# Top-1 expert layer over sorted tokens in groups of 1024 with weights gathered per tile, recurrence summed in PSUM, norm roots on GpSimd

## The reference

```python
px = x @ W_state.T + b_state ; g = sigmoid(x @ W_gate.T + b_gate)      # part 1
state = tanh(px_t + state) ; out_t = g_t * state                        # 256 steps, one after the other
top_id = argmax(x @ gate_w.T) ; score = sigmoid(max(x @ gate_w.T))      # part 2, E = 8 experts, F = 256
for e in range(8):
    xe = where(top_id == e, x * score, 0)
    acc += (silu(xe @ wg[e].T) * (xe @ wu[e].T)) @ wd[e].T
out = shared_swiglu(x) + acc
A = einsum('sbnq,sbnv->bnvq', unit(k), v * w)                           # part 3, 16 heads of 8
out = (einsum('sbnq,bnvq->sbnv', unit(q), A) * r) @ Wo.T + b
```

## Time and profile before

| | us |
|---|---|
| median of 3 runs (4196.43 to 4217.24) | 4210.99 |
| the profiled execution, its own time | 4206.35 |
| its span in the trace | 4204.6 |
| the first stage in it, 0 to the memset | 841 |
| what follows | 3363 |

### The profile page before, as it was taken

How to read it: one execution, slowest core, us unless ns; L and a number is a source line. 1 busy time by engine, 2 the same in 40 slices (tenths; PEclk the granted TensorE clock), 3 DMA queues, 4 the chain that set the end, 5 groups by cost and what they waited for, 6 DMA issues and landing times.

```text
span 4204.6 us, 149958 instructions
## 1 busy us (share of the span) xinstructions
PE 3830.9 (91%) x64432; PEld 2715.8 (65%) x64432; DVE 2923.7 (70%) x5136; ACT 2315.7 (55%) x4220; POOL 2929.8 (70%) x4274
## 2 busy tenths in 40 slices
PE   6989899778999899998999989999899998999997
PEld 3444444357777677776777767777677776777774
DVE  3566665567777677777777777777677776778672
ACT  3222211146666666666666666666666666666662
POOL 0122223288888788887888878888788887888782
PEclk9999999789999999999999999999999999999998
DMA  1000000011111111111111111111111111111110
GB/s 66 3 5 5 6 3 3 15 48 41 37 37 37 49 39 43 38 35 50 39 41 37 38 42 47 39 38 39 41 45 42 38 37 44 41 45 39 41 38 24
DMA packets 96277, 147.02 MB, mean 35 GB/s; under 512 B 27264, under 2 KB 35840, under 8 KB 95488
## 3 DMA queue, kind: packets, MB, share of 16 engines
q1 hardware_dynamic: 95616, 137.42, 13.0%
HBM read 32.46 MB, written 4.19 MB: 9 GB/s over the span
## 4 chain that ended last, share of the span: by engine, by line
PE 57%; POOL 26%; issue 8%; DVE 4%; ACT 2%; DMA 1%; SPq 1%; POOLq 0%; DVEq 0%; ACTq 0%
PE bank L445 12%; POOL m L1339 7%; PE bank L378 5%; PE bank L527 5%; PE bank L516 5%; POOL m L1333 4%; PE bank L489 4%; POOL S L1355 4%; PE bank L465 3%; PE bank L566 3%; POOL S L1347 3%; PE bank L455 3%; PE bank L500 3%; PE bank L393 2%; PE bank L574 2%
## 5 line engine op out<-in xcount | busy, mean ns | idle before, releaser
L445 PE MATMUL bank<-wqkv,xs 128*128 128x512 f32 x3456 | 1139.5, 446 | 16.3 <-DVE m L834 14.6
L1339 POOL TENSOR_TENSOR m<-m 128x512 f32<-128x512 f32 x768 | 966.5, 1279 | 47.6 <-DVE m L834 47.6
L445 PEld LDWEIGHTS bank<-wqkv,xs 128*128 128x128 f32 x3456 | 606.0, 195 | 179.3 <-issue 100.3
L832 DVE TENSOR_TENSOR m<-bank,tab 128x512 f32<-128x512 f32 x768 | 516.8, 673 | 132.5 <-ACT sq L1104 90.0
L844 DVE TENSOR_REDUCE ss<-sq 128x8 f32<-128x512 f32 x768 | 514.5, 677 | 120.4 <-ACT sq L1104 119.4
L834 DVE TENSOR_TENSOR m<-bank,tab 128x512 f32<-128x512 f32 x768 | 522.3, 680 | 35.8 <-POOL m L1339 35.7
L1104 ACT ACTIVATE sq<-bank 128x512 f32<-128x512 f32 x768 | 457.5, 596 | 130.7 <-PE bank L445 111.6
L1347 POOL TENSOR_TENSOR S<-S,nw 128x1024 f32<-128x1024 f32 x192 | 365.2, 1902 | 104.7 <-DVE S L864 104.6
L516 PEld LDWEIGHTS bank<-P,big 64*64 64x64 f32 x24576 | 376.2, 135 | 90.3 <-issue 89.7
L1355 POOL TENSOR_TENSOR S<-S,rs 128x512 f32<-128x512 f32 x384 | 392.9, 1044 | 39.1 <-DVE rs L878 38.8
L1112 ACT ACTIVATE vst<-bank 128x512 f32<-128x512 f32 x384 | 232.9, 606 | 328.2 <-PE bank L445 326.6
(11 more groups left out here) (202 smaller groups left out, 6586.6 us busy)
## 6 DMA issues: line engine op xcount, KB each, us to landing
big<-vst SPq DMA_DIRECT2D x1536, 64.0 KB, 2.0
stage<-in_wqkv SPq DMA_DIRECT2D x36, 256.0 KB, 2.9
tab<-in_tab SPq DMA_DIRECT2D x48, 128.0 KB, 2.2
big<-in_wa SPq DMA_DIRECT2D x1, 3460.0 KB, 12.8
wo<-in_wo SPq DMA_DIRECT2D x6, 512.0 KB, 3.7
big<-in_x SPq DMA_DIRECT2D x8, 256.0 KB, 2.9
keep<-Xr SPq DMA_DIRECT2D x8, 256.0 KB, 2.0
stage<-keep SPq DMA_DIRECT2D x8, 256.0 KB, 3.1
```

Of the source, the lines that this page charges most:

```text
L445: m = eng.matmul(pb[:, :], xt[a], wqkv[:, z, 512 * part:512 * part + 512], start=(n == 0), stop=(n == 2))
L832: eng.tensor_tensor(m1[:, part, :].rearrange("p (h d) -> p h d", d=DH), pv, ct.unsqueeze(1).to_broadcast([P, 8, DH]), ALU.mult)
L1339: eng.tensor_tensor(m1[:, part, :], m1[:, part, :], m2[:, part % 2, :], ALU.add).then_inc(s["g_add"], 1)
```

## The change

Parts 1 to 3 get another program; part 4 is the same.

- The experts work on sorted tokens. For a group of 1024 tokens (two chunks; GR = 4 groups) `rk` ranks them by expert: nine small matmuls (sums over tokens by a matrix of ones and by `below`, a triangle) and 13 small VectorE instructions give each token a slot so that each expert begins on a multiple of 128, in TL = 15 tiles. `xt` turns the tokens to rows and scales them; `sc` scatters them to DRAM by eight indirect DMAs of 128 rows; `lx` loads the sorted rows (SyncE, four DMAs). `wg` gathers the 128x768 weights of one tile's expert by an indirect DMA, into a ring of four; `tx` turns four tiles of tokens back to columns; `ge` is gate and up of two tiles, `he` silu, `ye` the down-projection, `ey` its copy to SBUF, `sy` a store to DRAM, `yg` eight indirect gathers that bring each token its row, and `cb` four matmuls by the identity that add it to the shared expert's output in bank 4. Expert weights are no longer all in SBUF.
- The recurrence has no VectorE part: for each step TensorE puts W_state times the column of x in a bank (`state_in`, 128x16) and adds the last state to it by a matmul with the identity; ScalarE's tanh reads PSUM and adds the bias.
- The root of each layer norm moves to GpSimd (`norm_root`, 12 small instructions), after a ScalarE copy; the widening copy of `fs` moves to ScalarE.
- `chunk_order()` is written anew: 7 rounds r of two halves; in half `now` = 2r or 2r+1 one chunk is in the recurrence, group r-1 in its experts (first half: ranks, scatter, tiles 0 to 5 and the gate of 6 and 7; second half: the rest and `yg`), and the chunks 2(r-2), 2(r-2)+1 in part 3. Each item has a place from -2 to 96, and a step is put in every third place or so.

```diff
-WA, WA_N = columns([("ws", 128), ("wg", 128), ("router", 8), ("sg", 256), ("su", 256), ("sd", 256),
-                    ("eg", E * 256), ("eu", E * 256), ("ed", E * 256)])
+WA, WA_N = columns([("ws", 128), ("wg", 128), ("router", 8), ("sg", 256), ("su", 256), ("sd", 256), ("below", 128),
+                    ("row", 1), ("tiles", 15)])
+GR, TL, PR = NC // 2, 15, 8
+SLOTS = 128 * TL
...
-    for p in range(-2, NC + 2):
-        gather = [
-            [("u", p + 1, 0), ("px", p + 2, 0), ("gu", p, 0), ("n2a", p - 1, 0), ("wv", p - 2, 0)],
-            [("gu", p, 1), ("n2b", p - 1, 0), ("n1a", p + 1, 0), ("wv", p - 2, 1), ("pm", p - 2, 0)],
-            [("gu", p, 2), ("n1b", p + 1, 0), ("wv", p - 2, 2), ("pm", p - 2, 1)],
...
+    for r in range(GR + 3):
+        for half in range(2):
+            e, a = r - 1, 2 * (r - 2)
+            done, now = 2 * r + half - 1, 2 * r + half
+            at = [(-2, "px", now, 0), (22, "pg", now, 0)] if now < NC else []
+            if 0 <= done < NC:
+                at += [(0, "u", done, 0), (3, "n1a", done, 0), (5, "n1b", done, 0), (8, "n1c", done, 0), (10, "ra", done, 0), (12, "xt", done, 0)]
+            if 0 <= e < GR and half == 0:
+                at += [(15, "rk", e, 0), (17, "sc", e, 0), (18, "lx", e, 0)] + [(18, "wg", e, j) for j in range(4)]
...
+            if 0 <= e < GR:
+                at += [(x[0], "wg", e, j) for x in at if x[1] == "ye" for j in (2 * x[3] + 4, 2 * x[3] + 5) if j < TL]
+            if 0 <= a < NC and half == 0:
+                at += [(2, "sh", a, 0), (4, "sh", a, 1), (7, "sd", a, 0), (7, "cb", a, 0), (9, "xr", a, 0), (11, "n2a", a, 0), (14, "n2b", a, 0),
+                       (17, "n2c", a, 0), (19, "fp", a, 0), (21, "fp", a, 1), (23, "fp", a, 2), (25, "fs", a, 0), (27, "fp", a, 3), (30, "fb", a, 0),
+                       (33, "fb", a, 1)]
+                at += [(36 + 8 * j, "wv", a, j) for j in range(8)] + [(45 + 8 * j, "pm", a, j) for j in range(7)]
...
+            taken = 0
+            for place, what, c, j in sorted(at, key=lambda x: x[0]):
+                while now < NC and taken < min(W, W * place // 95):
+                    yield "step", now, 0
+                    taken += 1
+                yield what, c, j
+            if now < NC:
+                yield "rest", now, 0
...
-        wa = big1
+        wa = big1[:, 0:WA_N]
+        wr = [big1[:, WA_N + 768 * i:WA_N + 768 * (i + 1)] for i in range(4)]
...
+                elif what == "lx":
+                    q.wait_ge("d_sc", 128 * (c + 1))
+                    q.wait_ge("p_tx", 4 * c)
+                    for n in range(4):
+                        eng.dma_start(XS[:, 4 * n:min(4 * n + 4, TL), :], rows_of(xsort_d, c, n)).then_inc(s[f"d_xs{n}"], 16)
+                elif what == "sy":
+                    q.wait_ge("a_y", PR * c + 2 * j + 2)
+                    eng.dma_start(rows_of(ysort_d, c, j), Y[:, 4 * j:min(4 * j + 4, TL), :]).then_inc(s["d_ys"], 16)
...
+            def state_in(n):
+
+                c, t = n // W, n % W
+                pe.wait_ge("a_rec", n - 1)
+                eng.matmul(bank[2 + n % 2][:, 0:NB], wa[:, WA["ws"]], bt(xin[c % 2])[:, :, t], start=True,
+                           stop=(n == 0)).then_inc(s["p_px"], 1)
+
+            def steps(c, first, last):
+                for t in range(first, last):
+                    n = W * c + t
+                    if n:
+                        prev = bt(hist[c % 2])[:, :, t - 1] if t else bt(hist[(c - 1) % 2])[:, :, W - 1]
+                        pe.wait_ge("d_kc", 32)
+                        pe.wait_ge("a_rec", n)
+                        eng.matmul(bank[2 + n % 2][:, 0:NB], ident, prev, start=False, stop=True).then_inc(s["p_st"], 1)
+                    if t < W - 1:
+                        state_in(n + 1)
...
+                elif what == "tx":
+                    pe.wait_ge(f"d_xs{j}", 16 * (c + 1))
+                    pb = claim(4)
+                    for n in range(4 * j, min(4 * j + 4, TL)):
+                        m = eng.transpose(pb[:, 128 * (n % 4):128 * (n % 4) + 128], XS[:, n, :], ident)
+                    m.then_inc(s["p_tx"], 1)
+                    vacant[4] = [("a_tx", 4 * c + j + 1)]
+                elif what == "ge":
+                    k = PR * c + j
+                    pe.wait_ge("a_tx", 4 * c + j // 2 + 1)
+                    pg, pu = claim(0), claim(1)
+                    for n in range(2 * j, min(2 * j + 2, TL)):
+                        g = TL * c + n
+                        pe.wait_ge(f"d_w{g % 4}", 16 * (g // 4 + 1))
+                        for pb, w0 in ((pg, 0), (pu, 256)):
+                            for f in range(2):
+                                a = 256 * (n % 2) + 128 * f
+                                m = eng.matmul(pb[:, a:a + 128], wr[g % 4][:, w0 + 128 * f:w0 + 128 * f + 128],
+                                               hX[j // 2 % 2][:, 128 * (n % 4):128 * (n % 4) + 128], start=True, stop=True)
+                    m.then_inc(s["p_ge"], 1)
...
+                elif what == "ye":
+                    k = PR * c + j
+                    pe.wait_ge("v_he", 2 * k + 2)
+                    pb = claim(4)
+                    for n in range(2 * j, min(2 * j + 2, TL)):
+                        a = 256 * (n % 2)
+                        for f in range(2):
+                            m = eng.matmul(pb[:, 128 * (n % 2):128 * (n % 2) + 128], hf[j % 2][:, a + 128 * f:a + 128 * f + 128],
+                                           wr[(TL * c + n) % 4][:, 512 + 128 * f:640 + 128 * f], start=(f == 0), stop=(f == 1))
+                        m.then_inc(s["p_ye"], 1)
+                    vacant[4] = [("a_y", k + 1)]
...
-                elif what == "gu":
-                    pe.wait_ge("v_xe", 8 * c + j + 1)
-                    for n in range(4):
-                        w0 = WA["eg" if n < 2 else "eu"].start + 256 * j + 128 * (n % 2)
-                        pb = claim(n)
-                        m = eng.matmul(pb[:, :], wa[:, w0:w0 + 128], xe[j % 2], start=(j == 0), stop=(j == E - 1))
-                        if j == E - 1:
-                            vacant[n] = [("v_gt", 4 * c + 2 * (n % 2) + n // 2 + 1)]
-                    m.then_inc(s["p_gu"], 1)
...
-                elif what == "dn":
-                    for f, name in enumerate(("v_hm", "g_hm")):
-                        pe.wait_ge(name, 8 * c + j + 1)
-                        w0 = WA["ed"].start + 256 * j + 128 * f
-                        eng.matmul(bank[4][:, :], wa[:, w0:w0 + 128], hm[(2 * j + f) % 4], start=False,
-                                   stop=(j == E - 1 and f == 1)).then_inc(s["p_dn"], 1)
+                elif what == "cb":
+                    pe.wait_ge(f"d_yt{c % 2}", 64 * (c // 2 + 1))
+                    for n in range(4):
+                        m = eng.matmul(bank[4][:, 128 * n:128 * n + 128], YT[:, 4 * (c % 2) + n, :], ident, start=False, stop=(n == 3))
+                    m.then_inc(s["p_cb"], 1)
...
-            def norm_b(k, c):
-                dv.wait_ge(f"p_n{k}v", c + 1)
-                eng.tensor_scalar(lv[:, k - 1, :], bank[7][:, 0:4], 1e-5, None, ALU.add).then_inc(s[f"v_n{k}"], 1)
-                rsqrt(lv[:, k - 1, :], lr[:, k - 1, 0, :], lr[:, k - 1, 1, :], f"v_n{k}", 11 * c + 1)
...
-            def steps(c, first, last):
-                for t in range(first, last):
-                    n = W * c + t
-                    if n:
-                        prev = bt(hist[c % 2])[:, :, t - 1] if t else bt(hist[(c - 1) % 2])[:, :, W - 1]
-                        dv.wait_ge("a_rec", n)
-                        dv.wait_ge("a_px", 2 * c + 1)
-                        eng.tensor_tensor(step_in[:, n % 2, :], bt(pP)[:, :, t], prev, ALU.add).then_inc(s["v_rec"], 1)
...
+                elif what in ("n1b", "n2b", "n3b"):
+                    k = int(what[1])
+                    ac.wait_ge(f"p_n{k}v", c + 1)
+                    ac.wait_ge(f"g_n{k}", 12 * c)
+                    eng.activation(lv[:, k - 1, :], bank[6][:, 0:4], ACT.Copy, scale=1.0, bias=0.0).then_inc(s[f"a_r{k}"], 1)
+                elif what == "fs":
+                    ac.wait_ge("v_fs", 11 * c + 11)
+                    ac.wait_ge("p_fb", 2 * c)
+                    eng.activation(wide.rearrange("p (h d) -> p h d", d=8), f_y.unsqueeze(2).to_broadcast([P, 128, 8]), ACT.Copy, scale=1.0,
+                                   bias=0.0).then_inc(s["a_wd"], 1)
...
+                    ac.wait_ge("p_st", n)
+                    eng.activation(h[:, :, t], bank[2 + n % 2][:, 0:NB], ACT.Tanh, scale=1.0, bias=ba[:, BA["bs"]]).then_inc(s["a_rec"], 1)
...
+            def norm_root(k, c):
+                nm, y, t, sem, n = lv[:, k - 1, :], lr[:, k - 1, 0, :], lr[:, k - 1, 1, :], s[f"g_n{k}"], 12 * c
+                wait = lambda m: po.wait_ge(f"g_n{k}", n + m)
+                po.wait_ge(f"a_r{k}", c + 1)
+                po.wait_ge(f"p_n{k}b", c)
```

(22 more changed lines are left out.)

378 lines of the change are left out of this document (201 added, 177 removed).

## The result

The changed kernel takes 4306.4 us (median of 4 runs, 4294.3 to 4315.6) against 4209.9 for the kernel before: ratio 1.023, 95% interval 1.019 to 1.027. I had forecast 4140, and the upper end of my range was 4225.

A forecast was written before the change was run, and what follows sets the result against it. TensorE was taken to bound the first stage. Its walk of 750 us plus 20 for the low clock gave 770, 71 less than 841, with the code behind unchanged: 4140 us, range 4065 to 4225.

The forecast's parts named there:

- What bounds the kernel, and what the change takes off TensorE: First stage: TensorE bounds it, 91.6 us a chunk with 11 of gaps; its work falls 17.8 us a chunk.
- The lone step, "0.68": Recurrence step with no other work between: matmul 0.36, tanh 0.23, 0.09 between, 0.68 us in all.
- The walk half by half: First stage walked in TensorE's order, items starting when bank and inputs are there: rounds 0 to 5 sum to 750 us.
- term of 17.5: Part 3, from projections to the first value product: 17.5 us, with 10 us of TensorE work in it.
- term of 20.5: Start of a round's first half: shared expert, norms 1 and 2 and ranks take 20.5 us.
- uncovered value product: Part 3: a value product that nothing covers takes 2.6 us, on VectorE and GpSimd.
- The 20 us for the low clock: First stage: 20 us added to the walk for TensorE at the low clock after long waits.
- Indirect DMAs: GpSimd's queue: 1.3 us per issue, 3.3 for a tile's weights to land; stage grows 56 us per us of issue.
- Norm roots: Roots moved to GpSimd: 3.5 us for 2.13 on VectorE, 1.6 us later, 24 times.
- A: Rival: first-stage waits nest as well as before, stage 700 us, whole 4069; chance 0.17.
- B: Rival: dear indirect DMAs on GpSimd's queue make the kernel slower, 4240 us at 3.1 each; chance 0.15.
- C: Rival: TensorE falls to the low clock or steps hold it; stage 815, or 841 without gain; chance 0.16.

The follow-up runs named there:

- e1: Changed kernel with the recurrence back on VectorE, one 512-column projection per chunk: 4247.1 us.
- e4: Changed kernel with the recurrence left out, one projection and one tanh per chunk, output not the reference's: 4206.2 us.
- e9: e8 plus an unread 472-column matmul ahead of 13 items a chunk in the serial stretches: ratio 1.001 to the kernel before.
- e8: Changed kernel with recurrence and norm roots both back on VectorE: 4237.5 us.
- e2: Changed kernel with an unread 256-column matmul added ahead of each step's input matmul: 4332.0 us.
- e5: e1 plus 26 unread 472-column matmuls a chunk, ahead of items that mostly wait: 4248.1 us.
- e13: Changed kernel plus 46 unread 472-column matmuls in the rounds without steps: 4297.0 us.
- e7: Changed kernel with all indirect DMAs made plain on SyncE's queue, fewer of them, weights not waiting for ranks, output not that of sorted tokens: 4252.0 us.
- e3: Changed kernel with the three norms' roots back on VectorE: 4304.1 us.
- e12: e8 plus the unread matmuls of e9 and the group-end gathers issued one at a time: 4198.6 us, ratio 1.000 to the kernel before.
- e6: Kernel before, with each expert gate and up matmul of 512 columns issued as four of 128: 4217.5 us.

## Why the prediction was wrong

*What bounds the kernel, and what the change takes off TensorE.* That TensorE bounds the kernel before held. Its 91.6 us a chunk mix the short first rounds with the later ones: the gate products of chunks 3 and 7 are 381.3 us apart, 95.3 a chunk. The instructions that were to leave TensorE did leave it, its busy time did not fall: 718 us in the stage before, 743 after, where 8 x 17.8 = 142 less was forecast. 127 us of the difference are the steps, whose matmuls (127.7 and 116.6 us busy for 511) took 0.48 us each in place of 0.23; how the other 40 us divide is not shown.

```profile
L354 PE MATMUL bank<-big 128*128 128x16 f32 x512 | 127.7, 328 | 4.1 <-DMA big<-in_x 4.1
L364 PE MATMUL bank<-big,kc 128*128 128x16 f32 x510 | 116.6, 309 | 11.2 <-ACT big L1080 11.2
```

*The lone step, "0.68".* It took 0.99 us at 1.2 GHz and 0.77 at 2.4. I had written that TensorE starts at its lower level and that a step costs some 0.9 there, and then walked round 0 with 0.68. That is 64 x 0.31 = 20 of the 25 us that round 0 ran over. e1 puts the whole form of the recurrence at 68 us.

*The walk half by half* is the step that failed most. Of 190 us too few, 59 lie in rounds 0 and 1, 69 in rounds 2 and 3, 63 behind the last step. The four halves of rounds 2 and 3 took 102, 92.5, 109 and 92 us against 83, 79, 86 and 79. e4 shows that rounds 2 and 3 are 49 us over the walk even with no steps, and the rest is 320 us long whatever the steps do. In each first half I had 38 us to the first value product, 20.5 for shared expert, norms and ranks and 17.5 for the projections; the rows at 620.7, 652.1 and 677.9 give 31.4 and 25.8. In e9, with the share at 0.86 there, the same stretch of the same chunks is 533.3 to 585.1, still 52 us:

```profile
563.46 1.81 PE L453 MATMUL bank<-big,qsb 128*128 128x512 f32 x2
...
585.13 1.26 POOL L1405 TENSOR_TENSOR gg<-big,Ar 128x512 f32<-128x512 f32 x1 [8.04 <-DVE Ar L877]
```

That is 30.1 us to the first projection and 21.7 from there to the value product, where e8, without the added matmuls, has 32.0 and 25.8. So the higher clock brought the term of 17.5 half of the way back, and left the term of 20.5, the larger miss, nearly as it was. I had let independent chains overlap freely, which I take for the reason: in TensorE's fixed order each item that waits holds the next chain back as well. One case is in the trace: the second norm's root is ready at 647.61, but its transposes start at 650.10 (the first line of the serial stretch), since they share bank 6 with the ranks, which VectorE reads until 649.95. How much of the miss such holds make up is not shown. An uncovered value product took (924.34 - 902.88) / 7 = 3.07 us, not 2.6; where the next chunk's shared expert and norm lay between, (874.50 - 845.37) / 7 = 4.2, and where tiles of experts did, (716.55 - 677.89) / 7 = 5.5:

```profile
902.88 1.26 POOL L1398 TENSOR_TENSOR gg<-big,Ar 128x512 f32<-128x512 f32 x1 [0.20 <-DVE Ar L867]
...
921.57 1.26 POOL L1398 TENSOR_TENSOR gg<-big,Ar 128x512 f32<-128x512 f32 x1 [1.19 <-PE bank L495]
924.34 1.26 POOL L1398 TENSOR_TENSOR gg<-big,Ar 128x512 f32<-128x512 f32 x1 [1.51 <-DVE Ar L867]
```

The part behind the last gate product I had walked at 257 us, what the kernel before takes for it (256), without ever comparing the two. There the new list has the experts of chunks 6 and 7 and all of part 3 of chunks 4 to 7 still to do, in pairs; the old one has the same two chunks' experts, but of chunk 4 only the value products and what follows them, and it goes on chunk by chunk. In every version with the new list this part stays at 296 us or more. How much of that lies in the grouping by two chunks no run here tells: the order of those rounds wasn't varied.

*The 20 us for the low clock* were too few. Three runs bear on it. e9 gains 25 us of stage net of 82 us of added work; in e2 82 us of work vanish in rounds 1 to 3; in e5 165 us vanish. A matmul left without cover waits and then takes twice as long (652.06 in the serial stretch). How much the clock costs in all can't be read off, because here whatever raised it added work. In e8 it lies above 25 us, and the 52 us of the stretch in e9 show that it isn't the whole 190. Behind the last step the raised clock gave little beyond the added work: 3 us in e9, 6 in e13.

*Indirect DMAs.* Right: 1.26 us each where I took 1.3; 61 us came back with plain ones where the sum made for e7 held 69, of fewer DMAs too, and with weights that no longer wait for the ranks. Weights landed in 4.4 us, not 3.3, and TensorE waited 21.8 us for them where I had about 25. `yg` cost 13 us, not 25. The issues took 0.95 to 0.98 us on average in each of their three groups: 0.98 for the 38 that had VectorE busy beside them for half of their time or more, 0.95 for the 69 that had it idle, 1.22 the longest. The Trainium skill ("SBUF — State Buffer", SBUF: two separate sides) says that such descriptors starve while VectorE runs a two-port instruction. No issue in this trace was held up in that way; whether a VectorE instruction beside one was of that kind it does not tell.

*Norm roots.* 12 instructions in 3.3 us (91.76 to 95.08 for the first), as priced; of 24 x 1.6 = 38 us 9 at most were on the path (e3).

*The rivals.* A was far off, the waits did not nest. B's mechanism was priced right and was not dear (its sum starts from 770, not 771). C named the place, and it was the nearest: the sign that it had set, long 512-column matmuls well after 100 us, came (2.07 us at 652). But its priced cases ended at 841, with a chance of 0.06 for more, and its first reason, the 16-column matmuls, was wrong: removing the steps left the share at 0.74. Level with the kernel before was the case of "nearly half of TensorE's work at 1.2 GHz"; by the share of 0.71 more than half of the time was, and the walk without the clock was already too short.

What stays open is how the excess of 190 us splits between the clock and the order of the list; the runs bound the first from below only. Settled is that neither the roots nor the steps made the clock, that the steps' form is worth 68 us and the indirect DMAs with the wait for the ranks 61, and that 64 of the 99 us which the changed kernel loses to the one before are lost where no step is left.

## What to carry to other kernels

A removed matmul was also cover: before counting its time as gained, list what waited behind it and price those waits exposed, in the engine's own order and at the lower clock. A list walked is checked against a stretch that the old trace shows in the same condition; here the last 72 us of the kernel before, alone at 0.72, were that stretch, and I had used them only for a term of 20 us. Start and end of a pipeline are walked apart and held against those of the old one; here the new end was 64 us longer than the old. Where waits can't be filled with useful work, a wide matmul that nobody reads can be worth more than it costs (e9), but here it brought the kernel no more than level with the one before (e9, e12).

## What the runs showed of the hardware

- TensorE busy is not TensorE fast: up to 126 us of the changed kernel it is busy about 0.8 of the time with 16-column matmuls and single items, and runs at 1.2 GHz. From 436.6 us on it runs at 1.2 GHz for 51 us in which no wait is longer than 2.1.
- Adding work raised the granted share from 0.74 to 0.83 (e9) and 0.86 (e5) at no cost or a gain. Splitting 512 columns into four times 128 with no wait between did not lower it: 0.96 for 0.94 (e6).
- The clock's column reads 1.00 before its first change is recorded, while a 512-column matmul takes 2.07 us there; the durations are what tells.
- An indirect DMA of 128 rows costs GpSimd 0.95 us and 0.30 between, for 512 bytes a row as for 3 KB; that VectorE was busy beside it added 0.03.
